# A six-layer local-attention stack on one Trainium2 core: 64-row score products, 96-query value products, single PSUM banks, two norms moved to GpSimd and four sequences in flight

## What is computed

```python
for i in range(DEPTH):                                   # 6
    x = attn_layer(shift_tokens(x), Wqkv[i], q_scale[i], k_scale[i], Wo[i]) + x
    x = ffn_layer(shift_tokens(x), ln_g[i], ln_b[i], W1[i], b1[i], W2[i], b2[i]) + x
# attn_layer: q, k, v = 16 heads of 64; q = l2norm(q) * qs, k = l2norm(k) * ksc; rotary with a scale
#   windows of 32 queries see 64 keys (their own window and the one before), masked; softmax; values; @ Wo
# ffn_layer:  layer norm, @ W1 + b1, a * gelu(gate), @ W2 + b2        (341 hidden)
```

## Time and profile before

| | |
|---|---|
| runs, median of 3 | 3597.83 us (3594.88 to 3600.31) |
| profiled execution, span | 3598.4 us |
| TensorE busy | 3482.8 us, 97% |
| VectorE busy | 3160.0 us, 88% |
| ScalarE busy | 3061.0 us, 85% |
| GpSimd busy | 2352.0 us, 65% |
| mean granted TensorE clock | 0.998 |

### The profile page before, as it was taken

The page is one execution under the profiler, slowest core; times in us unless marked ns, Lnnn a source line. Parts: engine busy times, 40 slices in busy tenths (PEclk is TensorE's granted clock), DMA queues, the critical chain, the costliest instruction groups (busy, mean ns, idle before and its releaser), DMA issues.

```text
span 3598.4 us, 95666 instructions
## 1 busy us (share of the span) xinstructions
PE 3482.8 (97%) x33868; PEld 2390.4 (66%) x33868; DVE 3160.0 (88%) x5848; ACT 3061.0 (85%) x5121; POOL 2352.0 (65%) x1607
## 2 busy tenths in 40 slices
PE   8999899999999999999999999999999999999998
PEld 6777466666666666666666666666666666666666
DVE  6998889888988988888888898888889888888986
ACT  5766688888888888888888888888888888888886
POOL 2001677777777777777777677777777777777774
PEclk9999999999999999999999999999999999999999
DMA  2000011112211112211112111112111112211112
GB/s 63 0 0 0 21 34 39 38 33 54 52 34 34 39 36 52 50 40 33 34 40 53 46 39 38 32 36 58 47 33 39 38 33 55 52 33 34 39 37 54
DMA packets 182965, 136.67 MB, mean 38 GB/s; under 512 B 97612, under 2 KB 135632, under 8 KB 182800
## 3 DMA queue, kind: packets, MB, share of 16 engines
q1 hardware_dynamic: 180019, 125.00, 14.8%
q10 hardware_dynamic: 2781, 9.51, 0.9%
HBM read 19.04 MB, written 2.10 MB: 6 GB/s over the span
## 4 chain that ended last, share of the span: by engine, by line
PE 62%; ACT 19%; issue 10%; DVE 5%; SPq 1%; POOL 1%; DMA 1%; ACTq 0%; DVEq 0%; POOLq 0%
PE ps L1302 12%; PE ps L1389 10%; PE ps L1356 10%; PE ps L1344 7%; PE ps L1379 4%; PE ps L1370 4%; PE ps L1160 3%; ACT L750 3%; ACT area L603 2%; DVE area L987 2%; ACT G L609 2%; ACT L609 2%; ACT area L618 2%; ACT area L625 2%; PE ps L1295 2%
## 5 line engine op out<-in xcount | busy, mean ns | idle before, releaser
L1302 PE MATMUL ps<-Wqkv,xsT 128*128 128x512 f32 x2304 | 1112.5, 605 | 8.7 <-ACT area L638 3.8
L449 POOL TENSOR_TENSOR area<-area,tab 128x512 f32<-128x512 f32 x768 | 970.0, 1273 | 146.7 <-ACT area L618 146.1
L1302 PEld LDWEIGHTS ps<-Wqkv,xsT 128*128 128x128 f32 x2304 | 391.2, 189 | 351.4 <-issue 295.0
L462 POOL TENSOR_TENSOR area<-area,lsum 128x1024 f32<-128x1024 f32 x192 | 365.5, 1904 | 383.2 <-DVE lsum L916 383.2
L456 POOL TENSOR_TENSOR AQb<-AQb,area 128x1024 f32<-128x1024 f32 x192 | 455.2, 2371 | 15.1
L456 POOL TENSOR_TENSOR area<-area 128x1024 f32<-128x1024 f32 x192 | 455.0, 2370 | 9.0 <-DVE area L976 1.5
L618 ACT ACTIVATE area<-ps 128x1024 f32<-128x1024 f32 x384 | 393.6, 1025 | 66.2 <-PE ps L1302 55.1
L1389 PEld LDWEIGHTS ps<-kbd,area 128*32 128x32 f32 x12288 | 313.2, 109 | 196.1 <-issue 113.4
L1344 PE MATMUL ps<-BD,area 128*64 128x128 f32 x6144 | 421.5, 279 | 17.7 <-issue 11.3
L1344 PEld LDWEIGHTS ps<-BD,area 128*64 128x64 f32 x6144 | 329.4, 137 | 158.8 <-issue 100.2
L1389 PE MATMUL ps<-kbd,area 128*32 128x128 f32 x12288 | 415.6, 276 | 17.0 <-ACT kbd L648 5.7
(11 more groups left out here) (136 smaller groups left out, 6630.6 us busy)
## 6 DMA issues: line engine op xcount, KB each, us to landing
BD<-area SPq DMA_DIRECT2D x1344, 64.0 KB, 2.0
Vx<-area SPq DMA_DIRECT2D x384, 32.0 KB, 1.9
Wqkv<-ffn_Wqkv ACTq DMA_DIRECT2D x18, 512.0 KB, 4.0
BB<-area SPq DMA_DIRECT2D x384, 16.0 KB, 1.8
x2s<-x2s SPq DMA_DIRECT2D x96, 56.0 KB, 2.0
Wo<-ffn_Wo SPq DMA_DIRECT2D x6, 512.0 KB, 4.3
W<-ffn_W SPq DMA_DIRECT2D x6, 341.0 KB
x2s<-x2s SPq DMA_DIRECT2D x96, 0.2 KB, 1.7
```

What stands on the lines that cost most here:

```text
L449: pool.tensor_tensor(b4[:, :, here], q4[:, :, there], s4[:, :, here], ALU.mult).then_inc((s_bq, s_bk)[j], 1)
L462: pool.tensor_tensor(p3, p3, lsum[:, 1, :].unsqueeze(2).broadcast_to([P, HEADS, 2 * WIN]), ALU.mult).then_inc(s_pn, 1)
L1302: last = mm(PJ[:, b * 512:(b + 1) * 512], xsT[:, par, t * P:(t + 1) * P], Wqkv[:, w0:w0 + 512], start=True, stop=True)
```

## The change

The stack alone is rewritten; the arithmetic is the same.

- **Scores:** the keys stand in `kT` without zeros (`kbd` is gone). One product is 64 rows by 32 queries with 64 key columns; the two heads of a pair use the two row halves and different banks. 64 products per tile, in one block for both halves of the heads.
- **Values:** one product is 64 keys by 64 channels with the 96 queries that can see those keys (64 at the end of the sequence). The band has three slots; `BB`, `Vx` and the edge products are gone. Four blocks of 16 per sequence.
- **Banks:** a table `HOME` gives every 512-wide result a single bank, so each projection is a product of its own with its own wait and its own 512-wide copy.
- **Norms:** for tile 0 `over_norms` runs on GpSimd; VectorE keeps tile 1.
- **Order:** the values move one step back and the feed-forward part two: n, n−1, n−2 and n−3 are in flight, 99 steps. All five engines' orders are new. The last steps have no `unread`.
- **Weights:** the halves of Wv are loaded apart.

```diff
-        kbd = sb("kbd", [P, PAIRS, 2, WIN + SEQ])
-        BD = sb("BD", [P, TILES, NWIN, HEADS, WIN])
-        BB = sb("BB", [P, 2, 4, 2, WIN])
-        Vx = sb("Vx", [P, 2, 2, P])
+        kT = sb("kT", [P, PAIRS, WIN + SEQ])
+        BD = sb("BD", [P, TILES, 3, HEADS, WIN])
...
+        HOME = {"x": 1, "xn": 7, "h0": 7, "h1": 0, "h2": 3, "y": 3, "out": 6,
+                "Q00": 0, "Q01": 1, "Q10": 7, "Q11": 4, "K00": 3, "K01": 0, "K10": 6, "K11": 4,
+                "V00": 5, "V01": 0, "V10": 7, "V11": 6,
...
+        SCORE_HOME = (5, 4)
+        VALUE_HOME = ((7, 0), (7, 1))
...
             def scores(n, t, g):
...
-                        last = mm(SC[32 * w:32 * w + 32, g, (c % 4) * P:(c % 4 + 1) * P],
-                                  qT[:, c, 32 * w:32 * w + 32], kbd[:, c, :, k0:k0 + 2 * WIN],
-                                  start=False, stop=True, skip_group_check=True)
+                        for k in range(2):
+                            half = slice(DH * k, DH * k + DH)
+                            last = mm(ps[32 * w:32 * w + 32, SCORE_HOME[k], 2 * WIN * c:2 * WIN * (c + 1)],
+                                      qT[half, c, 32 * w:32 * w + 32], kT[half, c, k0:k0 + 2 * WIN],
+                                      start=False, stop=True, skip_group_check=True)
...
+            def values(n, g, s, par):
+                for t in range(TILES):
+                    for pp in range(2):
+                        for k in range(2):
+                            for r in range(2):
+                                b = r ^ s
+                                c = 4 * g + 2 * b + pp
+                                h = 2 * c + k
+                                keys = slice(2 * WIN * r, 2 * WIN * (r + 1))
+                                wide = 2 if t and r else 3
+                                q0 = SEQ * pp + P * t + 2 * WIN * r
+                                last = mm(ps[DH * k:DH * k + DH, VALUE_HOME[g][b], q0:q0 + WIN * wide],
+                                          V[par][keys, t, h * DH:(h + 1) * DH], BD[keys, t, 0:wide, place(h), :],
...
+            def project(n, kind, part, par):
...
+                mm(home(kind + part), xsT[:, par, t * P:(t + 1) * P], Wqkv[:, w0:w0 + 512],
+                   start=True, stop=True).then_inc(done, 1)
...
+            def over_norms(n, j):
+                a3 = AQ[0][:, j * INNER:(j + 1) * INNER].rearrange("p (h d) -> p h d", d=DH)
...
+                pool.tensor_tensor(a3, a3, inv0[:, j * HEADS:(j + 1) * HEADS].unsqueeze(2).broadcast_to([P, HEADS, DH]),
+                                   ALU.mult).then_inc(s_n0, 1)
```

More of the change, by code:

```diff
@@ new lines, in step @@
+                if now:
+                    squares(n, 0, 1)
+                if three:
+                    gelus(n - 3, 1)
+                if one:
+                    turn_evac(n - 1, "q10")
+                    turn_evac(n - 1, "k10")
+                if now:
+                    keep_raw(n, 0, "10")
+                if three:
+                    gelus(n - 3, 2)
+                if now:
+                    keep_raw(n, 0, "11")
+                    if more:
+                        load_qkv(layer + 1, 0, d_wq)
@@ L767, in _ @@
+            stack_steps(act, step, 3)
         @block.vector
@@ L1041, in layer_norm, with step @@
                 last.then_inc(s_ln, 1)
-            def step(n, u, par, head, mid, ffn, layer, more=False):
-                if head:
+            def step(n, u, par, live, layer):
+                now, one, two, three = live
+                begin = isinstance(n, int) and n == 0
+                if now:
                     if isinstance(u, int) and u == 0:
-                        load_cosines(layer + 1 if n else 0)
+                        load_cosines(layer)
+                    if begin:
+                        a_residual(SEQS - 1)
@@ L1066, in step @@
+                if now:
+                    sum_q(n, 1)
+                if two:
+                    residual1(n - 2, u)
+                if now:
+                    sum_k(n, 1)
+                if one:
+                    soft_sum(n - 1, 1)
+                    turn(n - 1, 0)
+                if now:
+                    floor_norms(n, 1)
+                if three:
+                    residual2(n - 3, u, layer_of(u, 3, layer) == DEPTH - 1)
+                if two:
                     x2_moments(n - 2)
-                if mid:
-                    row_max(n - 1, 1, 0)
@@ L1461, in step @@
+                if one:
+                    need(pe, s_te, nth(n - 1, EVICTED, "q01"))
+                    turn(n - 1, "q00")
+                if now:
+                    project(n, "Q", "01", par)
+                    if begin:
+                        a_output(SEQS - 1)
                     if first:
                         pe.wait_ge(d_wk, loaded)
-                    project_k(n, 0, par)
-                if mid and not head:
-                    unread(4)
-                if mid:
-                    scores(n - 1, 1, 1)
@@ L1482, in step @@
[L1482 to L1491 removed]
+                    need(pe, s_x, SEQS + n - 3)
+                    project(n, "K", "00", par)
+                if one:
+                    need(pe, s_te, nth(n - 1, EVICTED, "q00"))
+                    project(n - 1, "V", "11", old)
@@ new lines, in step @@
+                if now:
+                    need(pe, s_hq, nth(n, PARTS["Q"], "00"))
+                    project(n, "K", "01", par)
+                if three:
+                    turn_xn(n - 3)
+                if one:
+                    scores(n - 1, 0)
+                if three:
+                    if static and u == 3:
+                        pe.wait_ge(d_ff, 16 * N_FF * (layer + 1))
+                    hidden(n - 3, 0)
+                if one:
+                    need(pe, s_nk, n)
+                    if static:
+                        need(pe, s_hq, nth(upto(n), PARTS["Q"], "01"))
+                    turn(n - 1, "k10")
@@ new lines, in step @@
+                if one:
+                    need(pe, s_te, nth(n - 1, EVICTED, "q10"))
+                    turn(n - 1, "q11")
+                if two:
+                    need_apart(pe, i_pe, s_half, 2 * (n - 2) + 1)
+                    values(n - 2, 0, 1, par)
+                if three:
+                    feed_out(n - 3)
+                if two:
+                    need_apart(pe, i_pe, s_te, nth(upto(n - 1), EVICTED, "k11"))
+                    need_apart(pe, i_pe, s_oe, 4 * (n - 2) + 1)
+                    values(n - 2, 1, 0, par)
@@ new lines, in step @@
+                if one:
+                    project(n - 1, "V", "01", old)
+                if now:
+                    need(pe, s_n0, 2 * n + 1)
+                    turn(n, "k01")
+                    need(pe, s_n0, 2 * n + 2)
+                    need(pe, s_r1, n - 1)
+                    if static:
+                        need(pe, s_hk, nth(n, PARTS["K"], "10"))
+                    turn(n, "q01")
+                    need(pe, s_ve, nth(n - 1, PARTS["V"], "01"))
+                    turn(n, "k00")
```

874 lines of the change are left out of this document (390 added, 484 removed), and 1 row of the table HOME.

## The result

The changed kernel takes **3467.62 us** (median of four, 3466.22 to 3473.4) beside 3597.03 for the kernel before on the same chip: ratio 0.964 [0.963, 0.966]. The forecast was 3308. The sign and the range held, the size did not: 129 us gained, not 289.

The account below looks back on a forecast made before the run. TensorE, 97% busy, was taken as the bound and expected to stay so. 371 ahead of the stack + 51.5 for two steps + 94 × 29.93 (2813.4) + 15 for layer changes + 57 drain = 3308 us; range 3220 to 3480.

Parts of the forecast that it names:

- Together 29.93, if the idle 0.87 stays: Steady step of the stack: 33.04 us falls to 29.93, with TensorE's idle 0.87 us a step unchanged.
- Scores, 1.01 a block: TensorE's score products: two new blocks at 1.01 us each replace four at 1.01, a gain of 2.02 us a step.
- the rest: TensorE's projections, `output`, `hidden`, `feed_out` and transpositions: unchanged but for some five more changes of kind, +0.25 us a step.
- Values, 0.80 a block: TensorE's value products: four blocks at 0.80 us, 3.18 against 4.52 before, a gain of 1.34 us a step.
- The bounds: Scores and values on TensorE: at best another 0.9 us gained; at worst 26.9 ns a record, 11.2 us against 8.56.
- Rival (b): TensorE cannot start small products fast enough: step 35.9 us, total 3872, deciding point 19 ns a record; chance 0.12 with both forms.
- First step 23: Step 0 of the stack: GpSimd's chain behind the first raw q takes 16 us, with tables and the start 23.
- Drain 57: End of the kernel: a third headless step comes in with less in each; kept at 57 us, bounds 50 to 70.
- Rival (a): Hand-overs of the three other engines set the step: 31.65 us if two GpSimd waits stay, total 3470; chance 0.15.
- Layer changes: Layer changes: Wv's second half is loaded at a step's end, other waits go; 15 us taken for 16.3.
- the copies to 512 columns: ScalarE's wide copies, six at 1.025 us, become 12 of 512 columns at 0.593; its step falls from 29.09 to 27.7.
- the order's slack: New order of a step: TensorE stays the bound, with 1 to 2 us of slack on each of three other engines.

Follow-up runs that it names:

- c_page_98: `a_pe_straight` with each TensorE step filled to 1024 instructions by satisfied waits in mid-step, and more ahead of the first stage: 3296.46 us, ratio 0.916.
- a_pe_straight: The changed kernel with TensorE's loops written out, the other engines keeping theirs: 3339.77 us, ratio 0.929.
- a_split_warm: `a_split` with 27 unread products ahead of the transposition of xn in each of the last two steps: 3365.95 us, ratio 0.936.
- a_split: `a_pe_straight` with each score block cut into two halves of 32 products and other TensorE work between them: 3359.19 us, ratio 0.935.
- a_norms_back: `a_pe_straight` with the two norms of tile 0 moved back from GpSimd to VectorE: 3695.35 us, ratio 1.028.
- b_pe_four: The kernel before the change, with four steps instead of two in TensorE's loop body: 3648.51 us, ratio 1.0145.
- a_body_1545: The changed kernel with its loops, scores of only one head of each pair computed in the loop steps: 3260.98 us, one execution.

## Why the prediction was right in sign and wrong in size

The books, forecast beside the runs (profiled executions):

| | forecast | after | `c_page_98` |
|---|---|---|---|
| ahead of the stack | 371 | 370.4 | 373.6 |
| first two steps | 51.5 | 27.7 + 27.4 | 29.4 + 27.2 |
| 94 steps with layer changes | 2828.4 | 2969.2 | 2795.9 |
| drain | 57 | 71.2 | 68.9 |
| sum | 3308 | 3465.9 | 3295.0 |

(From the last `turn_x`, at 3364.7 and 3196.5, to the end it is 101.2 and 98.5; I take a step of 30.0 and 29.6 off.)

- **"Together 29.93, if the idle 0.87 stays": the step is right, the idle is not.** Undisturbed steps are 29.0 to 29.8. This is the failed term: the idle time was carried over from the kernel before, with nothing for instructions that come late. The 94 steps took 2969.2 − 2828.4 = 141 us more than forecast, and that is a balance. Against the forecast stand the waits on issue (150 us in these steps, 134 in the window above), some 24 us of other waits, and the lower clock behind the stalls: the mean granted clock over 450 to 3200 us is 0.98, where the kernel before and `a_pe_straight` have 1.00. The trace has 89 us of that window at the lower level, so the clock cost up to 44 us, an estimate. In its favour stands the undisturbed step, which is shorter than 29.93. The forecast had a line for each engine and for the DMAs, but none for the instructions. That scores have 256 records a step for 128, and the kernel 51,488 for 33,868, stood in my sum as time only and not as code to be fetched. What the runs showed in its place: the loops written out give 128 us back, and with the page beginnings put right as well 171 (3467.62 to 3296.46).
- **Scores, 1.01 a block: measured 1.41 to 1.54.** Wrong by 0.4 to 0.5. The overlap read from rows 5 is there, but only the first 32 records run at its pace; rows 6, from which I read that streaming and not starting sets the pace, are the start of a block and say nothing of its 33rd record. The gain on scores is 1.0 to 1.1 and not 2.02 us.
- **Two opposite errors hid it.** From start to start, steps 66 to 79 of `a_pe_straight` (29.17 us) beside steps 4 to 13 of the kernel before (33.05): scores −0.96 (forecast −2.02), values −1.28 (−1.34), idle time 0.66 to 0.05 (forecast unchanged), and the rest −1.04, where I had put +0.25: turns 4.16 to 3.73, projections 10.97 to 10.61, `hidden` 2.92 to 2.70. That the undisturbed step came out near 29.93 is luck in its parts.
- **Values, 0.80 a block: 0.81 to 0.82.** Right.
- **The bounds, and the rule of the Trainium skill.** The records of L1357 start 6.9 and then 10.5 ns apart, not 26.9. The Trainium skill's floor of about 25 ns from start to start (TensorE: Matmul & The Clock Gate, "Wait — 56ns, not 53.3ns?") does not hold between records on eight tiles; the about 4 ns between tiles that the same page gives in its Part 3 is not reached as a mean: 6.9 at best. Rival (b)'s point of decision, 19 ns, was right as an account and the kernel lies on the fast side of it.
- **First step 23: 27.7.** It was not looked into beyond its length; with the second, at 27.4 for 28.5, it costs 3.6.
- **Drain 57: 71.** I named 70 as a bound but costed the third headless step at nothing. TensorE's waits after 3364 us in the changed kernel, and its clock from 3380:

```profile
PE ps L1289 <- DVE xn L1048: 14.9, 3, 6.9
```

```profile
3380.00:3466.00 86.00, 59.25 (x974) 46.76 (x972) 40.36 (x90) 41.44 (x70) 25.51 (x17) 0.86 0.20 51
```

  The excess is 14 us and this wait 14.9: with nothing else in the step, `turn_xn` waits 6.7 and 6.9 us for VectorE's normalised x. In the kernel before TensorE waits 0.6 us there and runs `unread` products ahead of it, so the two do not compare one to one, and what the third headless step costs by itself is not shown. The mean clock is 0.86 there, where it was 0.95. The unread products of `a_split_warm` raise it (from the last `turn_x` to the end 0.94, for 0.92 in `a_split`) and gain nothing, so I put the end down to the chain through VectorE.
- **Rival (a)** named 3470, and the result is 3467.6. The number fits, the cause does not: GpSimd and the others kept up, and with the instruction supply mended the kernel comes to 3296.46, within 12 us of the forecast, by the opposite errors above. `a_norms_back` shows how near that rival lay: the same norms in VectorE's order cost 356 us.
- **Layer changes, DMA, the copies to 512 columns, the order's slack:** the waits above show no term of a size worth naming.

## What to carry to other kernels

When a change turns one engine's work into more and smaller instructions, count that engine's loop body in instructions before pricing any of them: here a body that touched up to seven pages of 256 was kept and one of nine or more was fetched at every turn, and a jump in the instruction queue's packets (98 to 431) is the sign. If it does not fit, write the loop out, and then look where pages begin against dense stretches and waits, since moving three waits was worth 160 us. Waits that name no releaser point at the instruction supply before the order of the work.

## What the runs showed of the hardware that I had not expected

- TensorE's instructions arrive in pages of 256, 16 KB, a packet each. A packet takes 0.9 to 1.6 us, and 2.2 to 3.0 us pass from its start to the end of the stall that waits for it.
- At a loop's turn with a body of nine or ten pages, TensorE stands still for 2.6 to 3.6 us, in the third layer twice at one turn (3.1 and 2.8); with the 11 or 12 pages of `b_pe_four` for 1.5 to 2.4. With six or seven pages (the kernel before, four layers of `a_body_1545`) it never does.
- Such a stall is followed by the lower clock: 0.50 granted from 2081 to 2084 us, and 1.7 us more for six projection records.
- Whether a dense stretch (256 instructions in 1.4 us) stalls at a page's beginning depends on when the page's packet started, and waits several microseconds earlier move that: 0.6 us of lead and a stall, or 8 us of lead and none, with the page in the same place. In the blocks of scores no page with a lead of 1.9 us or more stalled.
- A satisfied wait is not free on TensorE: 190 more of them ahead of the first stage, about 95 instructions in the compiled program since they are packed in pairs, moved the first `turn_x` from 374.3 to 384.5 us, 0.1 us for each instruction.
- Eight 64-row by 32-column tiles overlap in full for the first 32 records of a block, eight records of 64 columns in 55 ns, where four on the column tiles alone take 53.8. From the 33rd record on one starts every 10.5 ns, and eight take 84.
